# Down-weight forms moved to VectorE, with two form buffers and the staged weights loaded in two halves

## What is computed

```python
x = x + xattn(layernorm(x), ctx, ctx)          # 8 heads of 16 channels, softmax over channels (q) and tokens (k)
Wg, Wu = NF4[gate_codes] * gate_scales, NF4[up_codes] * up_scales      # 2752 x 1024 each
Wd = NF4[down_codes] * down_scales                                      # 1024 x 2752
h = layernorm(x)
x = x + (silu(h @ Wg.T) * (h @ Wu.T)) @ Wd.T    # 2048 tokens in all
```

## Time and profile before

| | before |
|---|---|
| median of 3 runs | 1638.27 us |
| profiled execution | 1641.01 us, its span 1639.3 us |
| PE, PE weight loads, DVE, ACT busy | 1492.3, 1230.7, 958.4, 997.8 us |
| TensorE clock granted, mean | 0.954 |
| DMA | 303.23 MB, 185 GB/s |

### The profile page before, as it was taken

How to read it: one execution, slowest core, us unless ns; L and a number is a source line. 1 busy time by engine, 2 the same in 40 slices (tenths; PEclk the granted TensorE clock), 3 DMA queues, 4 the chain that set the end, 5 groups by cost and what they waited for, 6 DMA issues and landing times.

```text
span 1639.3 us, 18807 instructions
## 1 busy us (share of the span) xinstructions
PE 1492.3 (91%) x6804; PEld 1230.7 (75%) x6804; DVE 958.4 (58%) x1479; ACT 997.8 (61%) x1268; POOL 60.9 (4%) x99
## 2 busy tenths in 40 slices
PE   7999999999999998878879787798649999999999
PEld 7888888888888886656667666676538888888787
DVE  6986444443443332655556555565428878878765
ACT  5787998888888874666557565576413333333321
POOL 3343000000000000000000000000000000000000
PEclk9999999999999999988899988898879999999999
DMA  6554576666665767446455554555694443444341
GB/s 225 174 174 137 183 241 208 214 204 207 220 209 172 265 193 276 149 159 186 167 174 174 173 191 158 177 172 176 240 366 175 152 169 128 167 155 148 123 141 78
DMA packets 135708, 303.23 MB, mean 185 GB/s; under 512 B 9792, under 2 KB 57920, under 8 KB 130368
## 3 DMA queue, kind: packets, MB, share of 16 engines
q1 hardware_dynamic: 135616, 302.03, 55.4%
HBM read 189.27 MB, written 112.72 MB: 184 GB/s over the span
## 4 chain that ended last, share of the span: by engine, by line
PE 65%; DMA 14%; ACT 7%; DVE 7%; issue 3%; SPq 2%; ACTq 0%; DVEq 0%
PE bank L1494 10%; PE bank L1495 10%; PE bank L1493 10%; PE bank L1582 8%; PE bank L1584 7%; PE bank L1583 7%; DMA wf_scratch<-F 7%; DMA F<-w_scratch 5%; PE bank L1441 3%; PE bank L1539 2%; ACT F L808 2%; DVE R L1144 2%; PE bank L1540 2%; PE bank L1541 2%; DVE F L1144 2%
## 5 line engine op out<-in xcount | busy, mean ns | idle before, releaser
L1539 PE MATMUL bank<-R 128*128 128x512 f32 x604 | 253.5, 420 | 107.7 <-ACT F L885 63.3
L738 ACT ACTIVATE F<-F 128x1024 f32<-128x1024 f32 x294 | 311.9, 1061 | 9.3
L1493 PE MATMUL bank<-R 128*128 128x512 f32 x688 | 268.2, 390 | 0.0
L1494 PE MATMUL bank<-R 128*128 128x512 f32 x688 | 268.0, 389 | 0.0
L1495 PE MATMUL bank<-R 128*128 128x512 f32 x688 | 268.0, 389 | 0.0
L1540 PE MATMUL bank<-R 128*128 128x512 f32 x604 | 249.6, 413 | 0.0
L1541 PE MATMUL bank<-R 128*128 128x512 f32 x604 | 248.3, 411 | 0.0
L1144 DVE TENSOR_TENSOR F<-F 128x256 f32<-128x256 f32 (+2 forms) x305 | 169.4, 582 | 130.3 <-ACT F L857 127.5
L957 ACT COPY F<-bank 128x512 f32<-128x512 f32 x120 | 70.5, 588 | 268.9 <-PE bank L1584 268.1
L1539 PEld LDWEIGHTS bank<-R 128*128 128x128 f32 x604 | 122.5, 203 | 143.2 <-ACT F L885 67.1
L1144 DVE TENSOR_TENSOR R<-F,R 128x512 fp32r<-128x512 f32 (+2 forms) x215 | 164.9, 785 | 16.7 <-ACT R L872 16.5
(11 more groups left out here) (116 smaller groups left out, 2132.6 us busy)
## 6 DMA issues: line engine op xcount, KB each, us to landing
wf_scratch<-F SPq DMA_DIRECT2D x70, 512.0 KB, 3.1
F<-in_gu_scales SPq DMA_DIRECT2D x86, 256.0 KB, 3.9
inter_scratch<-F SPq DMA_DIRECT2D x84, 256.0 KB, 2.5
F<-w_scratch SPq DMA_DIRECT2D x21, 1024.0 KB, 8.2
FR<-wf_scratch SPq DMA_DIRECT2D x21, 1024.0 KB, 6.0
F<-in_gu_codes SPq DMA_DIRECT2D x41, 512.0 KB, 4.0
w_scratch<-F SPq DMA_DIRECT2D x41, 512.0 KB, 4.6
F<-inter_scratch SPq DMA_DIRECT2D x40, 512.0 KB, 3.7
```

The lines of the kernel that those rows point to most:

```text
L738: nc.scalar.activation(y, y, ACT.Prelu, bias=bias, scale=scale, alpha=alpha).then_inc(bent, 1)
L1493: pe.matmul(dst, hi, xh[:, tb, t, :], start=(t == 0), stop=False)
L1494: pe.matmul(dst, hi, xl[:, tb, t, :], start=False, stop=False)
L1539: pe.matmul(dst, hi, xform[i][:, 0, j, :], start=a, stop=False, skip_group_check=not start)
```

## The change

The high parts of the down forms are copied by DVE, right ahead of their low parts, and no longer by ACT. There are two form buffers, f(12) and the last eighth of R2, each with its own semaphore for its stores. The high parts of slices 5 and 6 of the gate and up weights are copied by DVE too; the low parts are made in the order 0, 1, 2, 3, 5, 4, 6. The staged weights are loaded in two halves, gate and up, ahead of the codes and scales in SP's queue. The block sums of the next position move one form earlier on DVE. At the start of the down stretch, two of the eight loads of y stand where six stood, `stage[1]` is f(18), and its load no longer waits for the stores of `inter`.

```diff
+        wdform = [form, [R2[:, 7 * N + q * WIDE:7 * N + (q + 1) * WIDE] for q in range(2)]]
+        wdform_out = [f(12), R2[:, 7 * N:8 * N].bitcast(F32)]
...
+        def made(p, i, those=range(NP)):
+            order = (0, 1, 2, 3, 5, 4, 6)
...
+        BY_ACT, BY_DVE = (0, 1, 2, 3, 4), (5, 6)
...
-        stage = [f(15), f(14)]
+        stage = [f(15), f(18)]
...
-            def load_staged(p):
+            def load_gate(p):
                 c = chunk_of(p)
                 if p:
-                    sp.wait_ge(wfl_ready, nth(p - 1, NP - 1))
...
+                    sp.wait_ge(wfl_ready, made(p - 1, 3))
+                    sp.wait_ge(ws_ready, p)
+                sp.dma_start(staged[:, 0:N], w_dram[GU - 1 if c == FULL else 2 * c]).then_inc(gate_in, 16)
+            def load_up(p):
+                if p == FPOS:
+                    return
+                if p:
+                    sp.wait_ge(wfl_ready, made(p - 1, 5))
+                sp.dma_start(staged[:, N:2 * N], w_dram[2 * chunk_of(p) + 1]).then_inc(up_in, 16)
...
+            load_gate(1)
             sp.wait_ge(up_done, ups_until(2 * FPOS + 3))
             load_xform(5)
+            load_up(1)
             load_xform(6)
             store_block(2 * FPOS + 3)
             for p in range(POS):
                 if p:
                     store_pair_out(p - 1, 1)
+                if p and p + 1 < POS:
+                    load_gate(p + 1)
+                    load_up(p + 1)
                 next_item(WN + 2 + p)
...
-                if p + 1 < POS:
-                    load_staged(p + 1)
                 for tb in range(4):
                     store_form(p, tb)
...
-                    for m in range(6):
+                    for m in range(2):
                         load_y(m)
                 store_pair_out(p, 0)
-            sp.wait_ge(pair_done, nth(FULL, NP - 1))
+            load_stage(1)
             store_pair_out(FULL, 1)
...
             load_w(0, 6)
-            for s in range(2):
-                sp.wait_ge(inter_stored[s], 2 * IN1)
-            load_stage(1)
-            for m in range(6, NM):
+            for m in range(2, NM):
                 load_y(m)
...
-            def form_hi(c, tb):
...
-                wait(act, form_stored, 16 * k)
-                nc.scalar.copy(form[0], src).then_inc(fh_ready, 1)
...
             def form_lo(c, tb):
...
+                wait(dve, form_stored[k % 2], 16 * (k // 2))
+                nc.vector.tensor_copy(hi, src).then_inc(fh_ready, 1)
                 dve.wait_ge(fh_ready, k + 1)
-                sub(form[1], src, form[0].bitcast(F32)).then_inc(fl_ready, 1)
+                sub(lo, src, hi.bitcast(F32)).then_inc(fl_ready, 1)
...
                 form_lo(p, 0)
+                if not last:
+                    weight_sums(p + 1)
                 form_lo(p, 1)
```

More of the change, by code:

```diff
@@ L262, in nth, with wform_source @@
             return sum(len(used(q)) for q in range(p)) + sum(j <= i for j in used(p))
+        def made(p, i, those=range(NP)):
+            order = (0, 1, 2, 3, 5, 4, 6)
+            own = [j for j in order if j in those]
+            until = order[:order.index(i) + 1]
+            return sum(j in own for q in range(p) for j in used(q)) + sum(j in own for j in used(p) if j in until)
+        BY_ACT, BY_DVE = (0, 1, 2, 3, 4), (5, 6)
         def fulls(p):
             return p if p <= FPOS else p - 1
+        def wform_source(p, i):
+            return {0: A11, 1: WS3, 3: A12, 6: WS4}[i] if p == FPOS else WFORMS[i]
         wslice = [R2[:, i * N:(i + 1) * N].rearrange("p (q n) -> p q n", q=2) for i in range(NP)]
@@ L616, in _ @@
                 if p == FULL:
-                    sp.wait_ge(wfl_ready, nth(p, NP - 1))
+                    sp.wait_ge(wfl_ready, made(p, NP - 1))
                     load_stage(0)
@@ L662, in _ @@
                     sp.wait_ge(wd_stored, 32)
+                    for q in range(2):
+                        sp.wait_ge(inter_stored[q], 2 * IN1)
                     sp.wait_ge(product_done, NP * g + 1)
@@ L867, in wform_hi @@
                 act.wait_ge(ws_ready, p + 1)
[L868 to L872, removed]
+                nc.scalar.copy(wslice[i][:, 0], wform_source(p, i)).then_inc(wfh_ready, 1)
             def snap1(p):
@@ L992, in _ @@
                 snap1(p)
-                form_hi(p, 0)
                 if last:
@@ L1157, in form_lo @@
             def form_lo(c, tb):
-                made = form_of(c, tb)
-                if made is None:
+                which = form_of(c, tb)
+                if which is None:
                     return
-                k, _, _, src, _ = made
+                k, _, _, src, _ = which
+                hi, lo = wdform[k % 2]
+                if k == 0:
+                    dve.wait_ge(xf_stored, 16 * xstored(XSTEPS))
+                if k % NP < 3:
+                    dve.wait_ge(w_ready, WN + c + 1)
+                else:
+                    dve.wait_ge(t_ready, 4 * (k // NP + 1))
+                wait(dve, form_stored[k % 2], 16 * (k // 2))
+                nc.vector.tensor_copy(hi, src).then_inc(fh_ready, 1)
                 dve.wait_ge(fh_ready, k + 1)
-                sub(form[1], src, form[0].bitcast(F32)).then_inc(fl_ready, 1)
+                sub(lo, src, hi.bitcast(F32)).then_inc(fl_ready, 1)
             def wide(v):
@@ L1215, in wform_lo @@
                     return
[L1216 to L1220 removed]
+                src = wform_source(p, i)
+                if i in BY_DVE:
+                    dve.wait_ge(*((pair_done, nth(p - 1, i)) if p else (up_done, ups_until(NB1 - 1))))
+                    dve.wait_ge(ws_ready, p + 1)
+                    nc.vector.tensor_copy(wslice[i][:, 0], src).then_inc(wfd_ready, 1)
+                    dve.wait_ge(wfd_ready, made(p, i, BY_DVE))
+                else:
+                    dve.wait_ge(wfh_ready, made(p, i, BY_ACT))
                 sub(wslice[i][:, 1], src, wslice[i][:, 0].bitcast(F32)).then_inc(wfl_ready, 1)
@@ L1305, in lo_s @@
                 dve.wait_ge(hs_ready, g + 1)
+                if g == 1:
+                    for s in range(2):
+                        dve.wait_ge(inter_stored[s], 2 * IN1)
                 sub(sform[g % 2][1], stemp.rearrange("p (a n) -> p a n", a=2), sform[g % 2][0].bitcast(F32)).then_inc(ls_ready, 1)
@@ L1368, in _ @@
                     pair_out(p - 1, 1)
-                for i in range(4, NP):
-                    wform_lo(p, i)
+                wform_lo(p, 5)
+                wform_lo(p, 4)
+                wform_lo(p, 6)
                 if p and not last:
@@ L1528, in pair_product @@
             def pair_product(p, i, dst, start, stop):
-                wait(pe, wfl_ready, nth(p, i))
+                pe.wait_ge(wfl_ready, made(p, i))
                 if p == 0:
```

55 lines of the change are left out of this document (19 added, 36 removed).

## The result

The changed kernel takes 1508.93 us, the median of 4 runs (1507.22 to 1512.88), against 1638.02 for the kernel before: a ratio of 0.9219, 95% interval 0.9189 to 0.9249. Forecast was 1503 with a range from 1478 to 1550. The profiled execution took 1512.88 and has a span of 1511.1 us, against 1641.01 and 1639.3.

The account below looks back on a forecast made before the run. Waits for form stores and staged weights were taken to hold pair positions at 25.4 us against PE's 19.0. Savings of 99 + 11 + 11 + 14 = 135 from 1641.0 gave 1506, as median 1503; range 1478 to 1550.

Parts of the forecast that it names:

- The copy: DVE's new 512-wide rounding copy in the pair stretch: 0.42 us, between bounds of 0.35 and 0.69.
- Odd position: Odd positions of the pair stretch: DVE's chain from result to result takes 18.8 us.
- Even position: Even positions of the pair stretch: DVE's chain takes 21.5 us, with the first form's store taken to land in 7.5.
- Positions 1 to 19: Main part of the pair stretch: 20.15 us per position instead of 25.4, saving 99 us.
- Position 0: First position of the pair stretch: staged weights land earlier, PE ends at 651.6 instead of 663.9; 11 us saved.
- Seam: From pair to down stretch: the second group's input is issued earlier, PE's product 4 starts sooner; 14 us saved.
- Positions 20 and 21: Last positions of the pair stretch: 36.2 us instead of 47.4, set by the first group's input; 11 us saved.
- The six loads of y behind: Down stretch: later y loads arrive in time, the third group's input close to when wanted; worth 1 us at most.
- Clock: Pair stretch: PE waits of 1 to 2.5 us in even positions cause no slow matmuls, an assumption.
- PE-bound: Rival, pair stretch: faster landings close DVE's waits, a position costs 19.1 us; 20 us more saved, 1483; chance 0.18.
- late-landing case: Rival, pair stretch: up lands at 9.4, the form store at 16.2; 22.45 us per position, 1547; chance 0.23.
- slower than before: Rival, pair stretch: DVE waits for stores, holding everything PE wants; 28.1 us per position with dearer copies, 1654; chance 0.02.

## Why the prediction was right

The time, the sign and the mechanism were right. In the pair stretch the mechanism was that DVE's waits for the weights' landing and for the first form's store set what a position lasts, a little above PE's own time. That the total came out within 6 us is partly luck, since one large error outside the pair stretch cancelled a smaller one inside it.

- **The copy.** 0.42 was taken between 0.35 and 0.69, and 0.42 was measured. That it fits to the hundredth is luck: the reason given was only "some fixed part".
- **Odd position.** 18.8 forecast, 18.84 in the one shown, 19.1 in the mean. It is below PE's own 19.04 and so can only make up for some of what an even one loses.
- **Even position.** 21.5 forecast, 20.7 in the mean of nine (19.7 to 22.1). The term that was mis-sized is the landing of the first form's store: 7.5 was taken, and the nine landed in 5.7 to 8.1 us, 6.7 in the mean. SP also issued it at 5.8 after T, not 6.2. So the third form's copy waits 1.1 to 1.7 us, not about 3. The sums start 7.5 after T in the mean, where 7.3 was taken, and their spread was not foreseen. The late landings of the weights fall in positions 2, 12, 15 and 18. In the trace of the changed kernel from the second chip positions 12, 15 and 18 are long again, so chance alone isn't likely. Why they are late stays open.
- **Positions 1 to 19**: 99 forecast, 104.7 measured, or 19.87 each for 20.15. (With nine even and ten odd positions the forecast's own terms give 20.08.) **Position 0**: 11 and 12.3. **Seam**: 14 and 13.2.
- **Positions 20 and 21**: 11 and 9.5. The first group's input was there 26.5 after T of position 20 (25.7 forecast), and from there to the last silu it took 10.6. The sum counted 8.75 for this, though its own row gave 10.2.
- **The six loads of y behind.** "Worth 1 us at most" was wrong: 10.8 us were given back. The prediction worked out neither when the third input lands nor when it is wanted. SP took 8 us to issue the six y and issued the input only after them; it landed 32 us after the pair stretch's end (1099.7 against 1067.8). ACT had waited for it since 1089.2. A product of the down stretch has 6 matmuls, not the 12 of a pair product, so that product 4 of the second group was due 25 us after that end (1101.11 - 8.51 = 1092.6). The experiment with the input ahead of y takes all of the 10.8 back, so this order was the cause.
- **Clock.** "At gaps this short no slow matmuls" held for nine of PE's ten waits for c22_sum in positions 1 to 19 (0.2 to 1.7 us), and not for the tenth, of 2.53 us (below).
- **The rivals.** PE-bound was not the case, but one DMA issue placed otherwise brings it about. Of the late-landing case the wait for the store existed, at 1.1 to 1.7 us per even position instead of the 3.2 of that case. That waits on DVE would make it slower than before did not happen: in odd positions no copy of DVE waited for a store. That rival also has a slip in its sum. If the last form starts at 22.8, the ledger's own 2.9 from there ends the position at 25.7, not 26.6, and at 27.2 with the dearer copies. By that it just misses the 27.3 from which it would have been slower.

The errors have both signs: 5.7, 1.3, -1.5 and -0.8 in the terms, -10.8 for the one left out, and -0.7 before position 0, where nothing was changed. They sum to 6.8 us of span.

What the prediction did not say, and only the experiments show, is which edits carry the gain. Taking the form copies off ACT, the edit that the change is named after, brings nothing. With all else as changed it costs 13 us in the positions and 17 to 20 by the ratios (0.920 and 0.9219 against 0.9096), until another store is placed ahead. The early loads and the second buffer carry the gain, neither of them more than about 40% of it alone (3.2% and 2.5% of some 8%). How much the earlier place of the block sums adds to that wasn't tried by itself. With one buffer it shows nothing: the changed kernel with one buffer (0.9685) and the kernel before with the early loads alone (0.9677) differ in the place of the sums, in who copies, in slices 5 and 6 and in the seam, and take the same time.

## What to carry to other kernels

When two landings are waited for in turn in one loop, mending one alone can show less than it is worth: measure them together before one is dropped. Where one queue issues transfers in order, put them in the order in which they are wanted, and look first at what a reused buffer waits for. Here, moving one 0.5 MB store ahead of 1 MB of codes and scales was worth 1%; in the changed kernel those were issued 16 us or more before their first use. Work in front of a wait for a landing cost nothing here, and taking it away only lengthened the wait.

## What the runs showed of the hardware

The granted clock went to its lower level after some short waits of PE and not after others. After a wait of 1.45 us the first matmuls of the changed kernel followed at full pace; after one of 2.53 us six were slow (timeline of PE, then a stretch of 1 us in which the third number from the end is the granted clock):

```profile
689.29 0.50 PE L1556 MATMUL bank<-R 128*128 128x512 f32 x1 [1.45 <-DVE F L1248]
689.62 0.39 PE L1557 MATMUL bank<-R 128*128 128x512 f32 x1
...
1006.54 0.79 PE L1556 MATMUL bank<-R 128*128 128x512 f32 x1 [2.53 <-DVE F L1248]
1007.13 0.63 PE L1557 MATMUL bank<-R 128*128 128x512 f32 x1
1007.56 0.63 PE L1558 MATMUL bank<-R 128*128 128x512 f32 x1
...
1007.00:1008.00 1.00, 1.00 (x4) 0.71 (x4) 0.23 (x2) 1.00 (x3) 0.00 (x0) 0.50 0.26 94
```

A granted clock of 0.50 is the lower of the two levels, 1.2 GHz, with matmuls 0.43 us apart instead of 0.23. In position 21 a wait of 3.31 us was followed by matmuls at full pace (granted clock 1.00 from 1063 to 1064) and only then by slow ones (0.50 from 1065 to 1067).

What is issued ahead of a transfer goes with how long it takes to land. The 0.5 MB store of a form landed in 3.1 us in the median. It took 5.7 to 8.1 us where codes and scales, 1 MB, had been issued right ahead of it, and in position 10 it took 3.6 where they had been issued behind it instead of 5.9.
